# A dynamic depthwise convolution on one Trainium2 core: the first image's statistics moved to VectorE, the taps scaled on VectorE, the later images' statistics placed later

## What is computed

```python
g = (x - mean(x, (2, 3))) / sqrt(var(x, (2, 3)) + 1e-5)       # per image and channel
avg = g.mean(axis=(2, 3))
wk = sigmoid(avg @ w1.T + b1).reshape(b * c, 1, 3, 3)
y = depthwise_conv(g, wk, padding=1) + conv_bias
out = x + (g - y) * fscale * g + y
```

## Time and profile before

| | |
|---|---|
| device time, median of 3 runs | 271.49 us (270.46 to 272.07) |
| the profiled execution: its time, its span | 272.44 us, 270.7 us |
| busy, share of the span: PE, DVE, ACT, POOL | 88%, 87%, 79%, 84% |
| DMA | 77.64 MB, mean 287 GB/s |
| the chain that ended last, by engine | POOL 65%, issue 14%, PE 12% |

### The profile page before, as it was taken

One profiled execution on the slowest core, in us unless ns is written; L12 is line 12 of the kernel. 1 busy time (PEld: TensorE's weight loads), 2 busy tenths in 40 slices (PEclk: granted clock), 3 DMA queues, 4 the chain that ended last, 5 costly groups with the idle time before them and its releaser, 6 DMA issues.

```text
span 270.7 us, 9000 instructions
## 1 busy us (share of the span) xinstructions
PE 237.2 (88%) x3506; PEld 183.5 (68%) x3506; DVE 236.0 (87%) x569; ACT 213.4 (79%) x386; POOL 227.5 (84%) x258
## 2 busy tenths in 40 slices
PE   0018997997999999999999999999999999999991
PEld 0014784785868686868677777868686877778670
DVE  2737789799999999999999999999999999755645
ACT  2116877698898989989898989898998989899520
POOL 0044266969999999999999999999999999999982
PEclk9999999799999999999999999999999999999999
DMA  7999901298498979799897979797979744444466
GB/s 262 336 404 426 402 30 68 110 338 372 170 353 324 353 296 367 282 357 351 292 399 261 385 278 381 298 362 290 372 277 374 319 177 178 176 178 174 179 274 251
DMA packets 10371, 77.64 MB, mean 287 GB/s; under 512 B 1265, under 2 KB 1496, under 8 KB 2648
## 3 DMA queue, kind: packets, MB, share of 16 engines
q1 hardware_dynamic: 10328, 77.06, 74.4%
HBM read 39.31 MB, written 37.75 MB: 285 GB/s over the span
## 4 chain that ended last, share of the span: by engine, by line
POOL 65%; issue 14%; PE 12%; DMA 4%; DVE 2%; SPq 1%; ACT 0%; POOLq 0%; DVEq 0%; ACTq 0%
POOL outs L841 46%; POOL inv_std L798 9%; PE conv_ps L426 7%; DMA gates<-gate 4%; PE conv_ps L432 2%; POOL tap L832 2%; POOL roots L824 1%; POOL avg L812 1%; POOL moments L808 1%; POOL square L806 1%; PE conv_ps L488 1%; POOL moments L803 1%; POOL numbers L822 1%; DVE outs L576 1%; SPq L314 1%
## 5 line engine op out<-in xcount | busy, mean ns | idle before, releaser
L426 PE MATMUL conv_ps<-xs,taps 64*64 64x448 f32 x1536 | 226.2, 555 | 2.5 <-DVE taps L550 1.5
L841 POOL TENSOR_TENSOR outs<-outs,linear 128x1152 f32<-128x1152 f32 x63 | 166.1, 2645 | 1.6 <-DVE outs L576 1.4
L432 PE MATMUL conv_ps<-xs,taps 64*64 64x128 f32 x1536 | 122.0, 273 | 0.0
L426 PEld LDWEIGHTS conv_ps<-xs,taps 64*64 64x64 f32 x1536 | 107.6, 134 | 20.3 <-issue 7.0
L576 DVE SCALAR_TENSOR_TENSOR outs<-xs,beta,conv_ps 128x576 f32<-128x576 f32 x128 | 102.6, 802 | 16.9 <-PE conv_ps L426 16.6
L713 ACT ACTIVATE linear<-xs,slope 128x576 f32<-128x576 f32 x128 | 109.4, 858 | 3.2 <-POOL outs L841 3.2
L432 PEld LDWEIGHTS conv_ps<-xs,taps 64*64 64x64 f32 x1536 | 102.1, 134 | 12.3 <-issue 6.1
L523 DVE BATCH_NORM_STATS2 pieces<-xs 128x6 f32<-128x64 f32 (+1 forms) x256 | 102.6, 451 | 5.1 <-DMA xs<-x 5.1
L688 ACT ACTIVATE xs<-xs,shift 128x594 f32<-128x594 f32 x128 | 99.4, 780 | 0.0
L798 POOL TENSOR_TENSOR inv_std<-numbers,minus_half 128x8 f32<-128x8 f32 x16 | 26.4, 1648 | 4.5 <-ACT dev_mean L694 4.5
L543 DVE TENSOR_TENSOR taps<-dyn_ps,tap 128x1512 f32<-128x1512 f32 (+1 forms) x19 | 27.9, 1481 | 2.1 <-POOL tap L832 2.1
(11 more groups left out here) (59 smaller groups left out, 153.7 us busy)
## 6 DMA issues: line engine op xcount, KB each, us to landing
xs<-x SPq DMA_DIRECT2D x30, 1188.0 KB, 11.0
out<-outs SPq DMA_DIRECT2D x30, 1152.0 KB, 5.2
xs<-x SPq DMA_DIRECT2D x4, 594.0 KB, 5.6
out<-outs SPq DMA_DIRECT2D x3, 576.0 KB, 2.9
out<-outs SPq DMA_DIRECT2D x2, 288.0 KB, 2.6
cst<-const SPq DMA_DIRECT2D x1, 248.0 KB, 7.0
w1s<-w1r SPq DMA_DIRECT2D x1, 115.9 KB
gates<-gate SPq DMA_DIRECT2D x1, 8.0 KB
```

Of the source, the lines that this page charges most:

```text
L426: return nc.tensor.matmul(tile(i, g, taken)[:, START:BANK], taps[given, i % 2, at:at + HALF], xs[given, i % XBUFS, g, 0:PAIRED, 1 + shift: ...
L432: return nc.tensor.matmul(tile(i, g, half)[:, BANK:END], taps[half, i % 2, at:at + HALF], xs[half, i % XBUFS, g, PAIRED:BLOCKS, 1 + shift: ...
L841: nc.gpsimd.tensor_tensor(tile, tile, linear[:, PAIR * k:PAIR * (k + 1)].rearrange("p g n -> p (g n)"), ALU.add).then_inc(out_ready, 1)
```

## The change

- **Loads.** Image 0 comes in eight pieces instead of four; `gates` goes ahead of `cst` and `w1s` and has a semaphore of its own; `w1s` is filled up with zero rows to 128.
- **Start.** `count`, `second_moments` and `average_columns` of image 0 move to VectorE (`first_count`, `first_moments`, `first_averages`). TensorE runs `keep_warm` matmuls (now 128 rows, 176 columns) from image 0's first piece on. No bn of image 2 runs ahead of the first product. Image 1's mean and spread move into the convolution of image 0 in the split form.
- **Taps.** `less_one` lies in PSUM, and VectorE scales the taps in `own_taps`; GpSimd's `scaled_taps` is gone.
- **Order from image 2 on.** TensorE: mean at 12 and 13 (was 9, 10), spread at 0 and 1 of the next image (was 13, 14), averages at 6 (was 3), dynamics at 8 and 9 (was 5, 6). VectorE: `rows(i+2)` behind product 3 and its bn, `own_taps(i+1)` and `matrices(i+1)` together behind product 4. GpSimd: `second_moments` behind `add_pair(i, 1)`, `deviation` and `average_columns` behind `add_pair(i, 2)`. ScalarE: `copy_stats` ahead of g1, `copy_averages` ahead of g4, `count` and `sigmoid` ahead of g6, `negative_mean` and `fill_margins` at the image's end. Images 1 and 2 have places of their own; bn of later images is spread as 10 in image 0, 12 in image 1 and 8 in each later image.

```diff
-WARM = 240
...
+WARM = 176
...
-FIRST_LOADS = 4
+FIRST_LOADS = 8
...
-    wr = np.concatenate([wr.reshape(TAPS * C, -1), br.reshape(TAPS, -1), other.reshape(SLOTS, -1)]).astype(np.float32)
+    rest = np.zeros((PARTS - INPUTS, GROUPS * SETS * SLOTS), np.float32)
+    wr = np.concatenate([wr.reshape(TAPS * C, -1), br.reshape(TAPS, -1), other.reshape(SLOTS, -1), rest]).astype(np.float32)
...
-        w1s = sb("w1s", [INPUTS, GROUPS * SETS * SLOTS])
+        w1s = sb("w1s", [PARTS, GROUPS * SETS * SLOTS])
...
-        less_one = sb("less_one", [PARTS, GROUPS * SETS])
...
+        less_one = dyn_ps[:, 384:384 + GROUPS * SETS]
...
             load_first()
+            sp.dma_start(gates[:].rearrange("p a g -> p (a g)"), gate).then_inc(gates_loaded, 16)
             sp.dma_start(cst[:], const).then_inc(consts_loaded, 16)
-            sp.dma_start(w1s[:], w1r).then_inc(params_loaded, 16)
-            sp.dma_start(gates[:].rearrange("p a g -> p (a g)"), gate).then_inc(params_loaded, 16)
+            sp.dma_start(w1s[:], w1r).then_inc(weights_loaded, 16)
...
-            pe.wait_ge(consts_loaded, 16)
...
+            MEAN = {1: (0, 2), 2: (1, 0), 3: (1, 14)}
+            SPREAD = {1: (0, 5), 2: (1, 4)}
+            AVERAGES = {1: (0, 10), 2: (1, 8)}
+            DYNAMICS = {1: (0, 11), 2: (1, 10)}
+
             def chain(i, at):
...
+                for j in range(i + 1, min(i + 3, B)):
+                    mean = MEAN.get(j, (j - 2, 12))
+                    spread = SPREAD.get(j, (j - 1, 0))
+                    dynamics = DYNAMICS.get(j, (j - 1, 8))
+                    if (i, at) == AVERAGES.get(j, (j - 1, 6)):
                         averages(j)
...
+                    if (i, at) == dynamics:
                         dynamics_first(j)
-                    if at == 6 + late:
+                    if (i, at - 1) == dynamics:
                         dynamics_second(j)
...
+                    if (i, at) == spread:
+                        spread_even(j)
+                    if (i, at - 1) == spread:
+                        spread_odd(j)
+                    if (i, at) == mean:
                         mean_even(j)
-                    if at == (12 if j == 2 else 10):
+                    if (i, at - 1) == mean:
                         mean_odd(j)
...
+            def keep_warm(weights, moving, count):
                 for _ in range(count):
...
+                    nc.tensor.matmul(conv_ps[:, CONV_TILES - 1, BANK:BANK + WARM], weights, moving, start=True, stop=True)
+
+            first = xs[:, 0, 0].rearrange("p k w -> p (k w)")
+            pe.wait_ge(first_loaded[0], 16)
+            for g in range(GROUPS + 1):
+                at_least(pe, pieces_done, g)
+                keep_warm(first[:, 0:PARTS], first[:, 0:WARM], 1)
+            pe.wait_ge(consts_loaded, 16)
+            still = (const_of("average"), cst[:, 0:WARM])
             mean_whole(0)
+            keep_warm(*still, 1)
             spread_whole(0)
-            keep_warm(3)
+            keep_warm(*still, 4)
             pe.wait_ge(last_columns_set, 1)
             averages_whole(0)
-            pe.wait_ge(params_loaded, 32)
+            pe.wait_ge(weights_loaded, 16)
             dynamics_whole(0)
-            keep_warm(2)
-            mean_whole(1)
-            keep_warm(1)
+            keep_warm(*still, 4)
...
-                dve.wait_ge(pieces_done, GROUPS * (j + 1))
...
             def own_taps(j):
                 dve.wait_ge(sig_ready, j + 1)
-                nc.vector.tensor_reduce(less_one[:], sig[:], AX_X, ALU.add).then_inc(less_one_ready, 1)
+                nc.vector.tensor_reduce(less_one, sig[:], AX_X, ALU.add).then_inc(less_one_ready, 1)
+                dve.wait_ge(roots_ready, j + 1)
+                dve.wait_ge(less_one_ready, j + 1)
+                nc.vector.tensor_tensor(tap[:], less_one.rearrange("p (g t) -> p g t", g=GROUPS),
+                                        roots[:, 1].unsqueeze(2).to_broadcast([PARTS, GROUPS, SETS]),
+                                        ALU.mult).then_inc(tap_ready, 1)
...
-            def first_matrices():
-                dve.wait_ge(tap_ready, 1)
-                last_column(0)
-                for k in range(PAIRS):
+            def first_matrices(first, last):
+                for k in range(first, last):
                     whole_triples(0, PAIR * k, PAIR * (k + 1))
...
+            def first_count():
+                dve.wait_ge(pieces_done, GROUPS)
+                nc.vector.tensor_scalar(pieces[:, 0, :, 1], pieces[:, 0, :, 1], const_of("counts"), None,
+                                        ALU.mult).then_inc(counted_ready, 1)
...
+            def first_moments():
+                dve.wait_ge(rows_done, 1)
+                dve.wait_ge(neg_mean_ready, 1)
+                nc.vector.tensor_tensor(moments[:, 0], row_stats[:, 0, :, 0], neg_mean_of(0), ALU.add).then_inc(dev_ready, 1)
+                dve.wait_ge(dev_ready, 1)
+                nc.vector.tensor_tensor(square[:], moments[:, 0], moments[:, 0], ALU.mult).then_inc(square_ready, 1)
...
+            def first_averages():
+                dve.wait_ge(zstats_copied, 2)
+                dve.wait_ge(r_ready, 1)
+                nc.vector.tensor_tensor(avg[:], dev_mean[:], inv_std[:, 0], ALU.mult).then_inc(avg_ready, 1)
+                dve.wait_ge(avg_ready, 1)
+                nc.vector.tensor_tensor(avg_cols[:, 0:TAPS * C].rearrange("p (a g) -> p a g", g=GROUPS),
+                                        const_of("spread")[:, 0:TAPS * C].rearrange("p (a g) -> p a g", g=GROUPS),
+                                        avg[:].unsqueeze(1).to_broadcast([PARTS, TAPS * SLOTS, GROUPS]),
+                                        ALU.mult).then_inc(avg_cols_ready, 1)
...
             dve.wait_ge(consts_loaded, 16)
+            first_count()
+            rows(0)
             nc.vector.tensor_copy(band_ps, const_of("band")).then_inc(constants_set, 1)
-            rows(0)
             nc.vector.tensor_copy(avg_cols[:, TAPS * C:], const_of("spread")[:, TAPS * C:]).then_inc(last_columns_set, 1)
+            nc.vector.tensor_copy(sig[:, :, SLOTS], const_of("centre")).then_inc(centres_filled, 1)
+            first_moments()
             dve.wait_ge(neg_f_ready, 1)
             nc.vector.reciprocal(inv_neg_f[:], neg_f).then_inc(inv_ready, 1)
-            nc.vector.tensor_copy(sig[:, :, SLOTS], const_of("centre")).then_inc(centres_filled, 1)
-            for g in range(GROUPS):
+            for g in range(4):
+                bn(1, g)
+            first_averages()
+            for g in range(4, GROUPS):
                 bn(1, g)
             dve.wait_ge(centres_filled, 1)
             own_taps(0)
+            dve.wait_ge(tap_ready, 1)
+            last_column(0)
+            first_matrices(0, 2)
             rows(1)
-            first_matrices()
-            for g in range(START_AHEAD):
-                bn(2, g)
-
...
+            first_matrices(2, PAIRS)
...
+            ahead = [(j, g) for j in range(2, B) for g in range(GROUPS)]
+
+            def bn_next(count=1):
+                for j, g in ahead[:count]:
+                    bn(j, g)
+                del ahead[:count]
...
+            def own_matrices(j):
+                own_taps(j)
+                matrices(j)
...
             for i in range(B):
                 nxt, stats = i + 1 < B, i + 2 < B
+                product(i, 0)
+                bn_next(2 if i < 2 else 1)
+                product(i, 1)
+                bn_next(2 if i < 2 else 1)
+                product(i, 2)
+                bn_next(2 if i < 2 else 1)
+                product(i, 3)
+                bn_next()
+                if stats and i > 0:
+                    rows(i + 2)
+                product(i, 4)
+                if nxt:
+                    own_matrices(i + 1)
+                bn_next()
+                product(i, 5)
                 if i == 0:
...
                     rows(2)
-                    bn(3, 0)
...
+                    bn_next()
+                product(i, 6)
+                bn_next()
+                if i == B - 1:
+                    add_last(GROUPS - 2)
+                product(i, 7)
+                bn_next(2 if i == 1 else 1)
             add_last(GROUPS - 1)
...
-            count(0)
...
             copy_stats(0)
-            centre(0, 1)
-            centre(0, 2)
+            for g in range(1, 5):
+                centre(0, g)
             copy_averages(0)
-            centre(0, 3)
-            centre(0, 4)
+            centre(0, 5)
             sigmoid(0)
+            centre(0, 6)
+            centre(0, 7)
             count(1)
-            for g in range(5, GROUPS):
-                centre(0, g)
             negative_mean(1)
             fill_margins(1)
+            COPY_STATS, COPY_AVERAGES, SIGMOID = {0: 2, 1: 3}, {1: 5}, {0: 5, 1: 7}
             for i in range(B):
                 nxt, stats = i + 1 < B, i + 2 < B
                 for g in range(GROUPS):
```

(49 more changed lines are left out.)

## The result

The changed kernel takes 278.95 us (median of 4 runs, 278.24 to 279.53). The ratio to the kernel before is on record as 1.026, with an interval of 1.023 to 1.029: 2.6% slower. The four runs of before beside it have a median of 270.98 us, and the two medians alone give 1.029, the upper end of the interval. Forecast were 275.7 us and 1.5% slower, in a range of 267.9 to 279.5. The sign and the mechanism were right; the loss was larger.

A forecast was written before the change was run, and what follows sets the result against it. Three engines share the bound, so a two-leg ring of hand-overs sets the turn. Turns +9.9, start -6.2, end +0.5 give +4.2 us: 276.6 profiled, 275.7 us median, 1.5% slower, range 267.9 to 279.5.

The forecast's parts named there:

- The ring: Middle, product 3 to the next image's product 3: two legs, 15.38 us a turn instead of 14.48; eleven turns +9.9 us.
- Leg A: Product 3 to product 5 of an image: VectorE's own list while TensorE waits, 6.05 us (5.85 to 6.2).
- the two own waits: VectorE between product 3 and product 5: reduction, scaling and filters wait for each other, 0.03 us per hand-over.
- Leg B: Product 5 to the next image's product 3: TensorE and the statistics, 5.95 + 3.38 = 9.33 us; before the change 9.69.
- TensorE behind GpSimd: After product 5: TensorE could start `averages` at 5.6 us, but GpSimd's pair, power and columns allow it only at 5.95.
- rival 2: Middle: GpSimd's way isn't in the ring, TensorE's is; turn 15.03 us, total 271.8 us, the same; chance 0.13.
- Rival 1: Middle: product 5 to product 3 stays VectorE's 8.64 us; turn 14.69, total 267.9 us, faster; chance 0.23.
- The later slots for `count` and `sigmoid`: ScalarE in each turn: costed at nothing, as ScalarE keeps 3 us free; otherwise each adds 0.2 to 0.4.
- Rival 3: Start: loads don't get better, image 1's first half lands some 5 us later; total 280.6 us; chance 0.06.
- the start: Up to product 3 of image 2: convolution starts at 21.1 us instead of 28.71; -6.2 us lasts (-7.7 to -3.2).
- The stretch from the convolution to product 3 of image 2: Start: from the first convolution at 21.1 us to product 3 of image 2 at 66.5 instead of 72.69.
- The stand of TensorE: Images 1 and 2: TensorE stands three times for some 2.5 us; 1.0 us (0 to 3) added for the clock falling.

The follow-up runs named there:

- without the power: Changed kernel with the power of the variance on GpSimd replaced by a multiplication from image 3 on: 274.7 us, ratio 1.011.
- the old order with the lead: Changed kernel with its start and VectorE taps, the earlier kernel's order from image 2 on, two bn more in image 0: 268.49 us, ratio 0.989.
- the run with 103 rows: Changed kernel with `w1s` loaded in 103 rows again, `gates` still ahead of it: 284.28 us, ratio 1.046.
- The two runs without the lead: Not singled out; three lack image 0's two extra bn: earlier order from image 2, 279.64 us; also GpSimd taps, 280.37; changed kernel, `rows` behind product 1, 278.69.

## Why the prediction was right, and where it was not

**The ring** held. The forecast turn was 15.38 us, measured are 15.39. Leg A: 6.05 forecast, 6.12 measured; the scaling, for which there was no row, was taken as 0.25 and takes 0.23, and the hand-overs within the two own waits are 0.10 and 0.04 us instead of the guessed 0.03. Leg B: 9.33 forecast, 9.25 measured; `averages` 5.95 and 5.91 after product 5. That the sum is right to 0.01 us is luck, as the misses of the two legs cancel; each leg is right to 0.1. Product 3's wait for TensorE is 0.44 us, where some 0.7 were expected.

**TensorE behind GpSimd** held as well: rival 2's turn, with TensorE alone, was put at 15.03, and without the power it is 15.09. Rival 1, VectorE's list as the bound (14.69), is what the old order with the lead gives: there, with `averages` early and `rows` and the reduction out of leg A, VectorE is the bound at 14.65. In the changed order it is out of reach, since product 3 waits 0.44 us for TensorE every time. The later slots for `count` and `sigmoid` cost nothing in a turn, as forecast: VectorE waits for neither in the middle. The reason given for it was wrong, as ScalarE does not keep 3 us free; the earlier trace rows has it busy for 13.21 of 14.57.

**Rival 3**, late loads, was put at 5 us; the run with 103 rows lost 4.75 us up to the first convolution, and all of it lasted to product 3 of image 2.

**The step that failed is the start**: up to product 3 of image 2 it gains 4.8 us instead of 6.2. The forecast let the first convolution begin at 21.1 us; it begins at 22.32. Most of it is one term: image 1's first half was put at 13.25 by the rate of image 0's pieces; it lands at 14.05, behind pieces that come slower. The bn of image 0, which were to end at 10.1, half a piece earlier than before, end at 10.97, as VectorE now waits for pieces; but VectorE then still waits 0.21 us for image 1, so that miss is hidden behind the other. From the reduction on 1.5 us were put down for 1.73, after a wait of 0.28 for the sigmoid that the forecast did not have (and 19.7 + 1.5 is 21.2, not 21.1). The profiled execution is not an odd one: with this start the first convolution begins at 21.46 to 22.46 us in ten runs, always after 21.1.

The stretch from the convolution to product 3 of image 2 was put at 45.4 us and is 45.6. In part that is luck, since in the five runs with the changed order it is 45.1 to 47.5. The stand of TensorE came, 2.79 us from 38.18 on, and behind it a granted clock of 0.50 from 41.6 to 44.9; no run separates what that cost from the 1.0 us allowed for it. One thing the forecast did not have: the first passes are slow for 2.2 us instead of 5.4.

**The other half of the miss** is not in any step. The forecast took the median to be 0.35% below the profiled execution, which was so for the runs of before; for the changed kernel it is 0.25% above. That is 1.6 of the 3.25 us between 275.7 and 278.95 (0.9 and 0.7); 1.4 are the start's. (The range's top, by its own terms, is 279.8 and not 279.5; the result lies below both.)

**Not foreseen** at all was that the chain's place and the lead of bn belong together. The forecast costed the new order as it is and did not ask what the old one had needed. The two runs without the lead look as if the order did not matter; the waits in their traces say why.

## What to carry to other kernels

Where three engines share the bound, find the hand-over that every turn goes through, cut the turn there, and sum each leg by rows: each sum was right to 0.1 us, though no engine's busy share told of it. A step may be moved to where its engine is idle only together with the lead of what feeds it; after every move look for a new wait, not at the time alone. On VectorE, keep one of two operands in PSUM when GpSimd works beside it.

## What the runs showed of the hardware

- Scaling 72 elements per partition on VectorE takes 0.23 us with one operand in PSUM, also beside an add_pair. With both in SBUF it takes 0.24 us while GpSimd is idle and 0.65 to 2.55 us beside an add_pair of GpSimd, as it lasts until that ends.
- A load of 103 rows, 116 KB, took until 16.04 us, where the same load in 128 rows took until 11.20. The last notice of image 1's halves behind it came 3.5 to 3.7 us after the one before (18.16 to 21.68 for the second half).
- TensorE's level at the first convolution is not the same from run to run. In the changed kernel a pass of 448 columns takes 0.95 to 1.01 us at first and mostly 0.53 to 0.54 later, which are the levels of 1.2 and 2.4 GHz. In the ten runs with the changed start, eight pieces, 128 rows of `w1s` and the `keep_warm` matmuls, the first convolution starts at 21.5 to 22.5 us and the first short pass at 21.46 to 24.68, so product 0 comes at 24.4 to 26.3. The column of the granted clock shows 1.00 through most of these slow stretches; the passes themselves have to be read. In the changed kernel TensorE was busy for 3.99 of the 4 us from 8 to 12 and for all of 20 to 24, and its passes were still slow at 22.32.
